# A graph layer on one core: row statistics issued in parts, 120 gathers ahead, carried sums kept in the rows

## What is computed

```python
edge_index = jnp.stack([src, dst])          # row = src, col = dst
h = jnp.maximum(_layernorm(x, axis=-1), 0.0)
deg = segment_sum(ones, row)                # how often a node is a src
deg_inv = where(deg > 0, rsqrt(max(deg, 1)), 0)
norm = deg_inv[row] * deg_inv[col]
msg = einsum('ebd,bdf->ef', comps[edge_type][:, :, None] * h[col][:, None, :], bases)
msg = msg * alpha[edge_type] * norm[:, None]
return x + segment_sum(msg, row)
```

## Time and profile before

| | |
|---|---|
| time, median of 3 runs | 754.39 us (753.51 to 755.52) |
| profiled execution, its time | 752.15 us |
| its span, first to last instruction | 750.2 us |
| busy: PE, DVE, ACT, POOL | 574.7, 596.4, 370.1, 540.3 us |
| mean granted TensorE clock | 0.927 of full speed |
| POOL scatters L393 | 196, 313.8 us busy |
| POOL gathers L372 | 196, 224.4 us busy |

### The profile page before, as it was taken

How to read it: one execution, slowest core, us unless ns; L and a number is a source line. 1 busy time by engine, 2 the same in 40 slices (tenths; PEclk the granted TensorE clock), 3 DMA queues, 4 the chain that set the end, 5 groups by cost and what they waited for, 6 DMA issues and landing times.

```text
span 750.2 us, 13642 instructions
## 1 busy us (share of the span) xinstructions
PE 574.7 (77%) x3922; PEld 406.0 (54%) x3922; DVE 596.4 (80%) x2624; ACT 370.1 (49%) x1494; POOL 540.3 (72%) x404
## 2 busy tenths in 40 slices
PE   4999985665676876987778788886797878888860
PEld 4666654443454645655556565655565656665430
DVE  7999995466775676886987899986998999998730
ACT  0345542244424678664545655645656534446530
POOL 3788886455555587778788888878878767767775
PEclk9999998687788899999998999999999999999995
DMA  8999999989833335444535455444455545544332
GB/s 272 287 326 339 331 361 323 319 296 327 307 101 81 70 54 122 79 92 69 109 52 100 92 86 95 96 81 95 82 95 96 92 78 78 86 57 82 35 36 25
DMA packets 56574, 108.89 MB, mean 145 GB/s; under 512 B 9339, under 2 KB 48264, under 8 KB 55684
## 3 DMA queue, kind: packets, MB, share of 16 engines
q0 software_dynamic: 34496, 25.72, 25.6%
q1 hardware_dynamic: 4416, 50.68, 18.7%
q10 hardware_dynamic: 17588, 31.62, 13.5%
HBM read 94.89 MB, written 64.61 MB: 213 GB/s over the span
## 4 chain that ended last, share of the span: by engine, by line
DVE 14%; DMA 13%; issue 10%; PE 9%; POOL 8%; ACT 7%; ACTq 0%; POOLq 0%
DMA out_dram<-acc,scatter_idx 11%; POOL out_dram L393 6%; DVE masked L481 4%; DVE part_sum L518 4%; PE pst L756 3%; PE pst L737 3%; DVE turned_hot L475 2%; POOL rows L372 2%; DVE same L537 2%; ACT acc L651 2%; DMA rows<-in_x_dram,dst_i 2%; DVE rows L518 2%; ACT scratch L603 2%; PE pst L764 1%; ACT scratch L595 1%
## 5 line engine op out<-in xcount | busy, mean ns | idle before, releaser
L393 POOL DMA_INDIRECT out_dram<-acc,scatter_idx x196 | 313.8, 1601 | 106.3 <-issue 53.7
L372 POOL DMA_INDIRECT rows<-in_x_dram,dst_i x196 | 224.4, 1145 | 96.4 <-issue 36.2
L737 PE MATMUL pst<-table_bits,turned_hot 128*128 128x198 f16 x1568 | 183.1, 267 | 84.0 <-DVE masked L481 61.1
L756 PE MATMUL pst<-bases_sb,h_turned 128*128 128x512 f32 x392 | 214.1, 629 | 0.0
L737 PEld LDWEIGHTS pst<-table_bits,turned_hot 128*128 128x128 f16 x1568 | 147.3, 105 | 113.6 <-issue 59.1
L518 DVE SCALAR_TENSOR_TENSOR part_sum<-pst,coef,part_sum 128x128 f32<-128x128 f32 x392 | 115.7, 343 | 96.2 <-ACT part_sum L641 89.3
L764 PEld LDWEIGHTS pst<-rows,same 128*128 128x128 f32 x392 | 73.0, 199 | 166.2 <-issue 152.1
L641 ACT ACTIVATE part_sum<-pst,coef 128x128 f32<-128x128 f32 x196 | 71.2, 363 | 183.4 <-PE pst L756 132.3
L481 DVE SCALAR_TENSOR_TENSOR masked<-iota_h,lo,pst 128x198 f32<-128x198 f16 x392 | 141.9, 415 | 20.9 <-PE pst L737 16.3
L764 PE MATMUL pst<-rows,same 128*128 128x128 f32 x392 | 82.7, 294 | 58.4 <-ACT acc L651 57.4
L651 ACT ACTIVATE acc<-pst,sum_scale 128x128 f32<-128x128 f32 x196 | 71.5, 365 | 58.5 <-DMA out_dram<-acc,scatter_idx 28.9
(11 more groups left out here) (71 smaller groups left out, 415.8 us busy)
## 6 DMA issues: line engine op xcount, KB each, us to landing
out_dram<-in_x_dram SPq DMA_DIRECT2D x46, 1000.0 KB
src_row<-src_rows ACTq DMA_DIRECT2D x25, 512.0 KB
edge_row<-edge_rows ACTq DMA_DIRECT2D x45, 256.0 KB
out_dram<-in_x_dram ACTq DMA_DIRECT2D x4, 1000.0 KB
rows<-in_x_dram,dst_i POOLq DMA_INDIRECT x196
out_dram<-acc,scatter_idx POOLq DMA_INDIRECT x196
rows<-edge_rows ACTq DMA_DIRECT2D x10, 175.0 KB
edge_row<-edge_rows SPq DMA_DIRECT2D x4, 256.0 KB
```

The costliest lines, as they stand in the source:

```text
L372: pool.indirect_dma_start(row(t), None, x, bass.IndirectOffsetOnAxis(ap=dst_i[:, t:t + 1], axis=0)) \
L393: pool.indirect_dma_start(out, bass.IndirectOffsetOnAxis(ap=scatter_idx[:, t:t + 1], axis=0), acc[:, t % ACC_RING, :], None, compute_op=AL ...
L737: last = pe.matmul(pst[:, LOOK + t % 2, k * LO:(k + 1) * LO], turned_hot[:, g % 2, c, k * W + j * P:k * W + (j + 1) * P], table[:, c * LO: ...
L756: pe.matmul(pst[:, PRODUCT + t % 4, :], h_turned[:, g % 2, j, :], bases_sb[:].rearrange("d b f -> d (b f)"), start=True, stop=True).then_i ...
```

## The change

- The statistics of a group are two functions, `row_sums(g)` and `row_squares(g)`. `stats_at(step, j)` deals the parts of a step's groups out over its four tiles and is called behind each tile's `first`, `keep_sum`, `keep_turned` and `relu`. With two groups in a step each tile gets one part (sums, squares, sums, squares); with one group the sums come behind tile 1 and the squares behind tile 3.
- POOL issues 120 gathers ahead of the first scatter. The gathers 56 to 119 are not paced by PE any more: ahead of each POOL writes a small tensor (`beat`, 128x40) twice and waits for its own write each time. Then `gathers_until(t)` is 120 + t/2.
- `keep_sum(t)` writes into `row(t)`, the scatter and the next `add_same` read it there. The ring `acc` and its wait for the scatter are gone.
- EDGE_RING is 5 instead of 4.

```diff
-    EDGE_RING = 4
+    EDGE_RING = 5
-    ACC_RING = 6
-    HIST_GATHERS = 56
-    LOOK_GATHERS = HIST_GATHERS + 4 * FIRST_LOOK * GROUP // 3
-    FIRST_GATHERS = LOOK_GATHERS + 3 * GROUP * SUM_STEP
+    HIST_GATHERS, FIRST_GATHERS = 56, 120
     def gathers_until(t):
-        return min(TILES, FIRST_GATHERS + (7 * t + 9) // 10)
+        return min(TILES, FIRST_GATHERS + t // 2)
@@ pace(t)
-                elif HIST_GATHERS <= t < LOOK_GATHERS:
-                    pool.wait_ge(look_ps, (t - HIST_GATHERS) * FIRST_LOOK * GROUP // (LOOK_GATHERS - HIST_GATHERS) + 1)
-                elif LOOK_GATHERS <= t < FIRST_GATHERS:
-                    tile, part = divmod(t - LOOK_GATHERS, 3)
-                    if part == 0:
-                        pool.wait_ge(product_ready, tile + 1)
-                    else:
-                        pool.wait_ge(look_ps, FIRST_LOOK * GROUP + 2 * tile + part)
+                elif HIST_GATHERS <= t < FIRST_GATHERS:
+                    for _ in range(2):
+                        beats[0] += 1
+                        pool.memset(beat[:], 0.0).then_inc(beat_ended, 1)
+                        pool.wait_ge(beat_ended, beats[0])
@@ scatter
-                                        acc[:, t % ACC_RING, :], None, compute_op=ALU.add) \
+                                        row(t), None, compute_op=ALU.add) \
@@ ScalarE
-            def stats(g):
+            def row_sums(g):
...
+            def row_squares(g):
                 act.wait_ge(row_summed, g + 1)
...
+            def stats_at(step, j):
+                a = STATS_BEFORE if step == 0 else stats_until(step - 1)
+                parts = [part for g in range(a, stats_until(step)) for part in ((row_sums, g), (row_squares, g))]
+                for part, g in parts[len(parts) * j // GROUP:len(parts) * (j + 1) // GROUP]:
+                    part(g)
@@ keep_sum(t)
-                if t >= ACC_RING:
-                    u = t - ACC_RING
-                    act.wait_ge(scattered[u % 2], 16 * (u // 2 + 1))
-                act.activation(acc[:, t % ACC_RING, :], pst[:, SUMS, 0:D], ACT.Copy, scale=sum_scale[:, t:t + 1]) \
+                act.activation(row(t), pst[:, SUMS, 0:D], ACT.Copy, scale=sum_scale[:, t:t + 1]) \
                     .then_inc(acc_ready, 1)
@@ main loop on ScalarE
-                for g in range(done_stats, stats_until(k)):
-                    stats(g)
-                done_stats = stats_until(k)
+                    stats_at(k, j)
@@ add_same(t)
-                                     acc[:, (t - 1) % ACC_RING, :], start=False, stop=True)
+                                     row(t - 1), start=False, stop=True)
```

More of the change, by code:

```diff
@@ L210, in build @@
         scatter_idx = sb("scatter_idx", [P, TILES], I32)
-        acc = sb("acc", [P, ACC_RING, D])
+        beat = sb("beat", [P, 40])
         pst = ctx.enter_context(nc.psum_tensor("pst", [P, 8, BANK], F32))
@@ L231, in build @@
         idx_ready = sem("idx_ready")
+        beat_ended = sem("beat_ended")
         type_row_loaded = [sem(f"type_row_loaded{b}") for b in range(TYPE_RING)]
@@ L351, in _ @@
                                pattern=[[1, P]], channel_multiplier=-1).then_inc(ident_ready, 1)
+            beats = [0]
             def pace(t):
@@ L667, in _ @@
                         load_types(act, i + TYPE_RING)
-                stats(g)
+                row_sums(g)
+                row_squares(g)
             batch, edge, rooted = 2, EDGE_RING, 1
@@ L673, in _ @@
             keep_turned(0)
-            done_stats = STATS_BEFORE
             for k in range(GROUPS):
```

## The result

The changed kernel takes 725.15 us (median of 4 runs, 723.03 to 726.71) against 754.95 (753.51 to 758.78) for the kernel before: a ratio of 0.9596, 95% interval 0.9552 to 0.9639. A second measurement gave 0.9615 (0.9574 to 0.9657). The profiled execution took 723.03 us with a span of 721.2. The forecast was 733, range 717 to 752: direction and range held, the gain came out at 30 us instead of 21.

What follows compares the result with a forecast made beforehand. POOL was taken as saturated from 320 to 590 us. Terms 12 + 11 - 2 + 2 = 23 us, taken as 21: 752.15 - 21 = 731 profiled, the median 2.2 above: 733, range 717 to 752.

Steps and rivals of the forecast that it cites:

- The bound: POOL saturated from 320 to 590 us, its pace of 11.6 us a step reaching the other engines.
- Start of the scatters, 228: 64 gathers from 112.68 us at 1.80 each, two 0.25 us beats included: first scatter at 228 instead of 212.6.
- The estimate that I had set beside the sum: Beats held up by each `turned_hots` on DVE: scatters start some 5 us later; left out of the sum.
- Scatters 0 to 39, 103 us from the start: POOL's 40 scatters and 19 gathers take 103 us; scatter 39 ends at 332 instead of 343.9, 12 us gained.
- my 13: From 205 to 320 us, the spread saves about half of DVE's 26.2 us of waits for `first`: 13 us.
- The wait for the edge row in step 1: The fifth edge row buffer takes away DVE's 3.75 us wait in step 1, or most of it.
- Scatters 40 to 151, 297 us: 28 steps of 10.6 us take 297 us instead of 307.6: 11 us gained, scatter 151 at 629.
- the coupling: Scatters 40 to 151: ACT's mid-step waits for gathers cost up to 4 us in two steps, taken as 0.2 a step.
- Lock step: Rival: ACT's mid-step gather waits make steps 12.4 us, time 782; slower from 11.4 a step; chance 0.10.
- that sign: POOL waiting more than 10 us for kept sums in scatters 40 to 151 would mean lock step.
- Scatters 152 to 195: Eight tiles take 20.5 us instead of 18.5, 2 lost; the last 36 scatters gain 0.06 each, 2 gained.

Runs made afterwards that it cites:

- experiment 5: The changed kernel with four beats instead of two ahead of each gather from 56 on; 747.75 us, ratio 1.0050 to the kernel before.
- experiment 6: The changed kernel with no beats and 132 gathers ahead instead of 120; 715.1 us, ratio 0.9591 to the kernel before.
- experiment 1: The changed kernel with a step's sums and squares back in one block behind its fourth tile; 730.5 us, ratio 0.9727 to the kernel before.
- experiment 8: The kernel before with gathers 56 to 107 paced by two beats each instead of waits for PE; 743.25 us, ratio 0.9874.
- experiment 3: The changed kernel with four edge row buffers instead of five; 724.35 us, ratio 0.9640 to the kernel before.
- experiment 4: The changed kernel, sums kept in the rows, but kept sum t waits for scatter t-6 again; 725.9 us, ratio 0.9682 to the kernel before.
- kernels with late gathers: The changed kernel with 132 gathers ahead, none beside scatters 0 to 28, then one with two; no beats 805.9 us, one beat 780.1 us.

## Why the prediction held, and where its sizes were off

**The bound.** Right in one direction. From its first scatter to the end of the looks POOL has no slack: in experiment 5 the 26 us at its start are 25 at the end. But from scatter 40 on it isn't the only bound: in experiment 6 15 us less work for it gained nothing there.

**Start of the scatters, 228.** Measured 218.1, 10 us early: the largest error. The term that was mis-sized is the price of a beat, 0.25 us by a write of 0.13 and a wait of 0.12. The write was right (0.13, the median of a single beat in experiment 5). What POOL adds to wait for itself is less, 0.07, so that a beat costs 0.20 (experiment 5); and a gather takes 0.96 in the median (0.98 in the mean) + 0.30, not 1.00 + 0.30. 64 x (1.80 - 1.66) = 9 us.

The estimate that I had set beside the sum by the Trainium skill (SBUF — State Buffer, Who interferes with whom) can be checked too. Of 128 beats 16 lasted 0.30 to 0.42 us instead of 0.13, and each of these 16 overlapped a `turned_hots` on VectorE, while only two of the 112 short ones did. The trace agrees with the exclusion that the page states; it costs 16 x 0.2 = 3 us here, where I had said 5.

**Scatters 0 to 39, 103 us from the start.** Measured 105.6. The kept sums were ready, the fortieth at 310.7 (I had 315). DVE's waits for `first` from 205 to 320 us fell from 26.2 to

```profile
DVE part_sum L514 <- ACT part_sum L646: 18.7, 12, 6.5
```

7.5 instead of my 13. That the spread is worth something here is shown by experiment 1: 14 us at the fortieth kept sum, some 8 at its scatter. The sums came early for another reason too, which I had not seen: step 0 itself starts 8 us earlier, as it does with the pacing alone (experiment 8). Scatter 39 ends at 323.7 and not at the 332 of the forecast because POOL starts 10 us earlier; the sums, 13 us ahead there, held it up for 1.2 us only. (Of the steps 0 to 4, which I gave as 22 to 25 us before the change, step 2 took 20.6.) The wait for the edge row in step 1, which I had priced at 3.75, is worth nothing that experiment 3 can tell.

**Scatters 40 to 151, 297 us.** Measured 298.7, and 298.6 to 300.3 in all ten profiles with one gather to two scatters; 307.6 to 308.8 in the four with seven to ten. The sum was right, one of its terms not: I had the engines at 10.4 us a step, from the seven steps of the earlier trace rows, and added 0.2 for the coupling. The fourteen steps 26 to 39 take 10.6 each in the kernel before and in the changed one, and 10.7 in experiment 6, so the last seven were a little cheaper than the 28 for which I used them (73.3 us in the changed kernel). The 10.6 came out by luck: what I had booked as coupling was in the steps themselves. And the 11.6 us a step that I gave for POOL's pace before are 11.5 by my own prices (4 x 1.93 + 2.8 x 1.34).

**Lock step.** Out. ACT stands before a group's missing gathers oftener, but not longer in total: 21.2 us from 320 to 590, against 25.9 in the earlier trace rows.

```profile
ACT scratch L591 <- DMA rows<-in_x_dram,dst_i: 21.2, 10, 9.9
```

POOL waits 7.1 us for kept sums in its 112 scatters in this trace, under the 10 that I had named, but 11.7 in the second trace of the same kernel (experiment 8), so that sign was a poor one. What rules lock step out is the length: 298.7 and 300.2 us, where it needed 319 or more. POOL isn't idle in fixed gaps alone, as I had said: it also waits 8.1 us in 12 waits for scatter t-2 to land. The 9.9 us of ACT are one wait, in step 11: there the engines give back the lead they had won ahead of scatter 39 (fortieth sum at 310.7, its scatter ended at 323.7).

**Scatters 152 to 195.** I booked 2 lost and 2 gained; measured 0.1 and 0.4 gained. The ring's waits in the earlier trace rows, 21.4 us, are gone and gave nothing, as experiment 4 shows with 44 us of them. They were what ACT did while POOL worked.

**The sum.** Forecast for the profiled execution 752.15 - 21 = 731, measured 723.0. Of the difference of 8, 10 are the start, 3 the other way lie between start and scatter 151 (105.6 + 298.7 against 104 + 297), the rest behind it and in rounding 23 down to 21.

**What stays open.** Why the first looks take 7 us longer in two of the three kernels in which POOL waits on PE's semaphores, and what holds VectorE for 20 us in the kernels with late gathers. The latter came on two chips on which the kernel without beats and with t // 2 did not run, so that the order of the later gathers and the chip are not told apart. The part that the sums in the rows play was not run alone; experiment 4 leaves it at nothing but the memory.

## What to carry to other kernels

Cut the span at the instructions of the engine that ends last, and keep a ledger of these stretches for each variant: here two classes, 299 and 308 us, showed at a glance which part did what. Waiting time of an engine that isn't the bound is no price list: 21 us of ring waits were worth nothing and 44 cost nothing, while 26 us at the start of the bound engine came out in full. And a bound is lowered only down to the next one, 10.6 to 10.7 us a step here, so work that is taken from POOL beyond that brings nothing there. Last, a ratio to the kernel before compares chips only as far as both kernels are slowed alike: a part is best run on the same chip as the whole.

## What the runs showed of the hardware that was not expected

How POOL's gathers are paced may change how fast other engines go. In one pair of kernels it did: with waits on PE's looks step 0 starts at 140.2 us, with POOL's own writes at 132.3, nothing else changed in the kernel; by time it was 1.3% on one chip. In a third kernel, with the same waits, the looks took no longer than with the writes (23.1 us from the first look to step 0, against 22.3). The mechanism was not found, and the chip is not ruled out.

While POOL gathers and the copies run, VectorE, TensorE and ScalarE stood still together in the two kernels with late gathers: in the first VectorE stood four times for 20 to 22 us before a pick, and the kernel with no beats took 84 us more than the changed one on the same chip (805.9 against 722.4). In another kernel, with the same gathers up to that point and no beats, but on another chip, step 0 started at 132.6 us. The DMA share does not tell them apart: from 130 to 210 us it is 0.88 in the kernel that stalls, 0.91 in this one and 0.96 in the changed kernel. The mechanism was not found.

A write of POOL took 0.34 us in the median (0.30 to 0.42) instead of 0.13 in the 16 cases in which it met a float16 one-hot of VectorE and was held up.
